# Two attention layers, a GRU and a last layer on one core: column tiles in the recurrent layer, a rebuilt variance in the last, one load moved up in the first

## The reference, cut to what matters

```
x = x + attention_0(x)          # 16 heads, softmax with mask
x = x + attention_1(x)          # 8 heads, queries are the keys
x = x + gru(h0=cond, inputs=x)  # 8 rows, 256 steps, width 512
    r = sigmoid(x_t W_r + b + h U_r + b);  z = sigmoid(x_t W_z + b + h U_z + b)
    n = tanh(x_t W_n + b + r * (h U_n + b)); h = (1 - z) * n + z * h
x = x + last(x, q=cond[1])
    blocks = x.reshape(8, 8 blocks, 32, 512).sum(axis=2)
    keys   = rms_normed(blocks @ Wk.T) * w;  a = softmax(keys @ q)
    proj   = (sum_n a_n blocks_n) @ Wo.T          # one row of 512 for each batch row
    y      = x + proj, then a layer norm over the 512 channels of every (batch, step)
```

## Time and profile before

| | us |
|---|---|
| median of 3 runs | 2085.04 |
| lowest, highest | 2074.66, 2086.17 |
| profiled execution: its own time | 2081.26 |
| profiled execution: span, first to last instruction | 2079.5 |
| attention, from 0 to the switch | 1006.5 |
| recurrent layer, 1006.5 to 2009.7 | 1003.2 |
| last layer, 2009.7 to the end | 69.8 |

### The profile page before, as it was taken

The page is one execution under the profiler, slowest core; times in us unless marked ns, Lnnn a source line. Parts: engine busy times, 40 slices in busy tenths (PEclk is TensorE's granted clock), DMA queues, the critical chain, the costliest instruction groups (busy, mean ns, idle before and its releaser), DMA issues. The chain is left out here.

```text
span 2079.5 us, 75171 instructions
## 1 busy us (share of the span) xinstructions
PE 1932.3 (93%) x32564; PEld 1312.7 (63%) x32564; DVE 1141.3 (55%) x3355; ACT 790.4 (38%) x2131; POOL 394.7 (19%) x867
## 2 busy tenths in 40 slices
PE   4788999999999999998899999999999999998777
PEld 2333444444444444444788888888888888887755
DVE  3535667575757566724255555555555555555546
ACT  0344555565646565653222222222222222222224
POOL 0011121111121202110212222212222221222103
PEclk7768999999999999997999999999999999999995
DMA  4525343442524251322300000000000000000002
GB/s 129 191 69 153 82 145 91 115 120 85 149 77 143 79 153 47 94 59 86 115 11 11 12 12 4 11 12 11 12 11 10 5 12 12 12 11 12 4 3 81
DMA packets 64616, 127.37 MB, mean 61 GB/s; under 512 B 14425, under 2 KB 21209, under 8 KB 60692
## 3 DMA queue, kind: packets, MB, share of 16 engines
q1 hardware_dynamic: 61212, 121.74, 19.9%
q0 software_dynamic: 3072, 0.82, 0.2%
HBM read 77.56 MB, written 37.85 MB: 55 GB/s over the span
## 5 line engine op out<-in xcount | busy, mean ns | idle before, releaser
L391 DVE TENSOR_REDUCE mx<-MX 128x1 f32<-128x512 f32 x768 | 486.6, 685 | 221.6 <-PE MX L511 221.0
L900 PE MATMUL gate<-whh,state 128*8 128x128 f32 x16384 | 496.3, 273 | 40.5 <-DVE state L823 28.9
L447 ACT ACTIVATE pr<-ST 128x512 f32<-128x512 f32 x768 | 412.2, 600 | 179.1 <-PE ST L531 178.2
L900 PEld LDWEIGHTS gate<-whh,state 128*8 128x8 f32 x16384 | 422.0, 91 | 89.6 <-DVE state L823 89.0
L511 PE MATMUL MX<-K,Q 51*128 51x512 f32 (+1 forms) x768 | 251.7, 478 | 25.7 <-DMA Q<-d_rows 19.5
L900 PE MATMUL pg<-whh,state 128*8 128x128 f32 x8192 | 270.8, 273 | 0.0
L801 DVE STREAM_TRANSPOSE trn<-gate 128x128 f32<-128x128 f32 x256 | 81.2, 317 | 338.1 <-PE gate L900 338.1
L852 ACT ACTIVATE rg<-pre 128x32 f32<-128x32 f32 x256 | 58.8, 230 | 541.4 <-DVE pre L803 541.3
L531 PE MATMUL ST<-Q,K 53*128 53x512 f32 (+1 forms) x768 | 247.0, 495 | 13.4 <-ACT pr L447 11.7
L531 PEld LDWEIGHTS ST<-Q,K 53*128 53x128 f32 (+1 forms) x768 | 101.2, 190 | 216.5 <-ACT pr L447 119.7
L900 PEld LDWEIGHTS pg<-whh,state 128*8 128x8 f32 x8192 | 223.7, 90 | 0.4
(11 more groups left out here) (166 smaller groups left out, 1940.9 us busy)
## 6 DMA issues: line engine op xcount, KB each, us to landing
d_q<-hi_q SPq DMA_DIRECT2D x32, 256.0 KB
d_q<-lo_q SPq DMA_DIRECT2D x32, 256.0 KB
d_k<-hi_k SPq DMA_DIRECT2D x32, 256.0 KB
d_k<-lo_k SPq DMA_DIRECT2D x32, 256.0 KB
K<-d_k SPq DMA_DIRECT2D x64, 128.0 KB
Q<-d_q SPq DMA_DIRECT2D x64, 128.0 KB
K<-d_k SPq DMA_DIRECT2D x16, 512.0 KB
Q<-d_q SPq DMA_DIRECT2D x16, 512.0 KB
```

Source lines behind the costliest of these rows:

```text
L391: dve.reduce_max(mx[:, u, col:col + 1], bank[:, :], AX.X).then_inc(mx_red, 1)
L447: act.activation(pr[:, kc % 2, i], ST[n % 3][:, :], ACT.Exp, scale=SCALE[UNITS[w][0]]).then_inc(exped, 1)
L900: last = pe.matmul(bank[32 * j:32 * j + B, lo:hi], held[q][:, c, :], whh[:, c, o + lo:o + hi], start=first, stop=done)
```

## The change

The diff, cut to its core:

```diff
--- before.py
+++ after.py
                     second_layer(it, 0)
-                else:
+                load_in(it + 2)
+                if not there(it):
                     sp.dma_start(xT[:], xt_in).then_inc(xT_in, 16)
                     preload(sp)
-                load_in(it + 2)
                 if there(it):
...
-        TG, TZ, RZ = 32, 16, 3
+        TG, TZ, RZ = 16, 16, 3
...
-        PIECES_Z = [(i, w, n) for i in range(TG // TZ) for w in range(C) for n in range(C)]
-        assert len(PIECES) == len(PIECES_Z) == TG
+        PIECES_Z = [(n, w, k) for n in range(1, NZ) for w in range(C) for k in range(C)]
+        Z_AT = [min(2 * t if t < TZ else TZ + t, len(PIECES_Z)) for t in range(T + 1)]
+        KEPT_Z = {next(t for t in range(T) if Z_AT[t + 1] >= C * C * n): n for n in range(1, NZ)}
+        T0 = T - TG
+        PARTS_AT, MEANS_AT = {T0 + 2 * n: n for n in range(last)}, {T0 + 1: 0, T0 + 3: 1, T0 + 6: 2}
+        CENTRE_AT = {T0 + 2 + n: divmod(n, C) for n in range(C * last)}
+        MU = (gb[1], zb, gb[1], gb[1])
...
+                pool.wait_ge(s_z_ev, 1)
+                pool.tensor_tensor(giZ[0][:], giZ[0][:], bz[:, 0], ALU.add).then_inc(s_z0, 1)
...
+                    if t in CENTRE_AT:
+                        blk, c = CENTRE_AT[t]
+                        dve.wait_ge(f_mu, blk + 1)
+                        dve.tensor_tensor(xa[:, blk, c], MU[blk][:, :], chunk(c, blk), ALU.add).then_inc(f_c, 1)
...
-                    last = pe.matmul(gb[i % 2][:, 0:TG * B], wih[:, n, i * P:(i + 1) * P],
-                                     xT[:, n, TG * blk:TG * (blk + 1), :].rearrange("p t b -> p (t b)"), start=n == 0, stop=n == C - 1)
+                    for j in range(4):
+                        last = pe.matmul(gb[i % 2][32 * j:32 * j + 32, 0:TG * B], wih[:, n, i * P + 32 * j:i * P + 32 * j + 32],
+                                         xT[:, n, TG * blk:TG * (blk + 1), :].rearrange("p t b -> p (t b)"), start=n == 0, stop=n == C - 1)
...
-                    i, w, n = PIECES_Z[k]
-                    t0 = TG * blk + TZ * i
-                    if w == 0 and n == 0 and t0 > 0:
-                        pe.wait_ge(s_z_ev, t0 // TZ)
-                    last = pe.matmul(zb[:, P * w:P * (w + 1)], xT[:, n, t0:t0 + TZ, :].rearrange("p t b -> p (t b)"),
-                                     wihZ[:, n, P * w:P * (w + 1)], start=n == 0, stop=n == C - 1)
-                    if w == C - 1 and n == C - 1:
+                def piece_z(n, w, k):
+                    if w == 0 and k == 0 and n > 0:
+                        pe.wait_ge(s_z_ev, n)
+                    for j in range(4):
+                        t0 = TZ * n + 4 * j
+                        last = pe.matmul(zb[32 * j:32 * j + 32, P * w:P * (w + 1)], xT[:, k, t0:t0 + 4, :].rearrange("p t b -> p (t b)"),
+                                         wihZ[:, k, P * w:P * (w + 1)], start=k == 0, stop=k == C - 1)
...
+                    if t == 0:
+                        pe.wait_ge(s_z0, 1)
+                    elif n > 0 and v == 0:
+                        pe.wait_ge(s_zd[n % RZ], 192 * (n // RZ + (0 if n % RZ == 0 else 1)))
...
+                        if n == 0:
+                            pe.matmul(psZ[t % 2][32 * j:32 * j + B, 0:P], identz[:, B * v:B * v + B], giZ[0][:, P * j:P * (j + 1)], start=True, stop=False)
+                            continue
...
-                        piece(blk + 1, k)
-                        piece_z(blk + 1, k)
+                        piece(blk + 1, 2 * k)
+                        piece(blk + 1, 2 * k + 1)
+                    for n, w, c in PIECES_Z[Z_AT[t]:Z_AT[t + 1]]:
+                        piece_z(n, w, c)
+                    if t in PARTS_AT:
+                        blk = PARTS_AT[t]
+                        if blk == 0:
+                            pe.wait_ge(s_gi_ev, PER * NG)
+                            pe.wait_ge(s_z_ev, NZ)
+                        else:
+                            pe.wait_ge(f_kept, blk)
+                        pe.wait_ge(s_acc, TB * (blk + 1))
+                        for c in range(C):
+                            mm = pe.matmul(gb[0][32 * c:32 * c + 32, :], mean[:, 0:32], chunk(c, blk), start=True, stop=True)
+                        mm.then_inc(f_part, 1)
+                    if t in MEANS_AT:
+                        blk = MEANS_AT[t]
+                        pe.wait_ge(f_kept, blk + 1)
+                        if blk == 2:
+                            pe.wait_ge(f_c, C)
+                        pe.matmul(MU[blk][:, :], fold[:], parts[:, blk], start=True, stop=True).then_inc(f_mu, 1)
...
+                def turn(blk):
+                    dve.wait_ge(f_var, blk + 1)
+                    if blk >= 2:
+                        dve.wait_ge(f_vf, blk - 1)
+                    dve.transpose(turned[:, blk % 2].rearrange("p w r -> p (w r)"), VB[blk % 2][:, :]).then_inc(f_vt, 1)
...
                 shift(0)
-                for c in range(C):
-                    centre(1, c)
                 shift(1)
-                for blk in range(NBLK):
-                    spread(blk)
-                    if blk + 2 < NBLK:
-                        for c in range(C):
-                            centre(blk + 2, c)
-                        shift(blk + 2)
-                    scale(blk)
+                turn(0)
+                shift(2)
+                spread(0)
+                turn(1)
+                scale(0)
+                shift(3)
+                spread(1)
+                turn(2)
+                scale(1)
+                spread(2)
+                turn(3)
+                scale(2)
+                spread(3)
+                scale(3)
...
+                def halves(bank, w):
                     for c in range(C):
-                        mm = pe.matmul(bank[32 * c:32 * c + 32, :], mean[:, 0:32], chunk(c, blk), start=True, stop=True)
-                    mm.then_inc(f_part, 1)
-                def means(blk):
-                    pe.wait_ge(f_kept, blk + 1)
-                    pe.matmul(MU[blk][:, :], fold[:], parts[:, blk], start=True, stop=True).then_inc(f_mu, 1)
-                pe.wait_ge(f_ld, 80)
+                        for j in range(2):
+                            mm = pe.matmul(bank[64 * j:64 * j + 64, 0:HD], br[:, c].rearrange("p n b -> p (n b)"), w[:, c, HD * j:HD * (j + 1)],
+                                           start=c == 0, stop=c == C - 1)
+                    return mm
...
                 def var(blk):
                     pe.wait_ge(f_sq, C * (blk + 1))
                     if blk >= 2:
-                        pe.wait_ge(f_sd, blk - 1)
-                    for g in range(4):
-                        for c in range(C):
-                            mm = pe.matmul(VC[blk % 2][:, g:g + 1], sq[:, blk % 2, c, g * P:(g + 1) * P], ones[:, 0:1], start=c == 0, stop=c == C - 1)
+                        pe.wait_ge(f_vt, blk - 1)
+                    for c in range(C):
+                        mm = pe.matmul(VB[blk % 2][32 * c:32 * c + 32, :], mean[:, 0:32], sq[:, blk % 2, c], start=True, stop=True)
                     mm.then_inc(f_var, 1)
+                def together(blk):
+                    pe.wait_ge(f_vt, blk + 1)
+                    o = 384 + W * blk
+                    pe.matmul(SP[0:32, o:o + W], pick32[:], turned[:, blk % 2, :, 0], start=True, stop=True).then_inc(f_vf, 1)
...
                 square(0)
                 square(1)
-                for blk in range(NBLK):
-                    root(blk)
-                    shifted_by_beta(blk)
-                    if blk + 2 < NBLK:
-                        square(blk + 2)
+                shifted_by_beta(0)
+                root(0)
+                square(2)
+                root(1)
+                shifted_by_beta(1)
+                square(3)
+                root(2)
+                shifted_by_beta(2)
+                root(3)
+                shifted_by_beta(3)
...
```

271 lines of the change are left out of this document (137 added, 134 removed).

## The result

The changed kernel takes 2053.16 us in the median of 4 runs (2046.30 to 2062.89), the kernel before 2083.41 in the same runs: ratio 0.987, interval 0.982 to 0.991. In two further sets it was 0.986 (0.984 to 0.988; 2050.80 against 2079.55 us) and 0.989 (0.987 to 0.991; 2060.13 against 2081.69). The profiled execution has 2051.92 us of its own and a span of 2050.1, 29.3 us less than before.

| stage | before | changed | difference | predicted |
|---|---|---|---|---|
| attention, up to the switch | 1006.56 | 990.15 | -16.4 | -10.0 |
| switch to the first scan | 24.72 | 19.86 | -4.9 | -8.6 |
| steps 0 to 15 | 61.60 | 64.32 | +2.7 | +2.2 |
| steps 16 to 254 | 915.36 | 917.32 | +2.0 | +0.6 |
| keys to `pm` | 19.10 | 12.45 | -6.7 | -5.5 |

What follows compares the result with a forecast made beforehand. It took an `xin` wait, pieces made ahead, the 3.83 us step chain and the last layer as limits. -10.0 - 8.6 + 2.8 - 5.5 - 10.1 = -31.4 us on 2081.3 gave 2050 us, range 2035 to 2067.

Steps and rivals of the forecast that it cites:

- Part 1: First layer: the load of `xin` issued earlier removes TensorE's whole 10.28 us wait; -10.0 us.
- bound of -11.5: First layer: the most the moved load was to gain, in us, as the low clock may rise earlier too.
- Rival B: First layer: TensorE later waits for a stack behind `xT`, giving back up to 10 us; 2060 us, chance 0.15.
- Part 2: Start of the recurrent layer: 48 groups of pieces at 0.26 us take 12.5 us instead of 21.1; -8.6 us.
- Part 3: Recurrent steps: +2.2 us in steps 0 to 15, +0.6 from three `means`; +2.8 us, bounds 0 and +6.
- 0.14 us a step: Steps 0 to 15: four groups and a longer `begin` take 1.24 us, 0.14 over the room; +2.2 us.
- The `means`: Steps 241, 243 and 246: wide products with 512 columns overrun the room by 0.2 us each; +0.6 us.
- Rival A: Recurrent layer: strips' weight loads run in series, a group costs 0.434 us; 2111 us, chance 0.05.
- Part 4: Last layer, keys to `pm`: a chain of 13.6 us in place of 19.1; -5.5 us, bounds -7.5 and -3.
- Part 5: Last layer, `pm` to last addition: walking DVE's and ACT's lists gives 36.9 us in place of 47.0; -10.1 us.
- rival D: Last layer: DVE's and ACT's list is longer than walked, 4 to 8 us less gain; 2056 us, chance 0.13.
- Clock C: Last layer: the clock stays up behind `pm` instead of falling to half; 2046 us, chance 0.10.

Runs made afterwards that it cites:

- e1: Kernel before the change with only the load of the next input moved ahead of xT and preload; 2066.60 us, ratio 0.993 to before.
- e2: Changed kernel with the old order of loads, so all of the change but the load's move; 2068.96 us, ratio 0.994 to before.
- e3: Changed kernel with the 3 MB load of the recurrent weights issued only once the first update block is kept; 2049.78 us in one run.
- e5: Changed kernel with the pieces in 128 weight columns again instead of strips, in steps of 16; 2054.79 us in one run.
- e9: Changed kernel with GpSimd's last-layer additions cut from 512 columns to 8, leaving out most of the last sum; 2056.62 us in one run.
- e6: Changed kernel with ScalarE's first root in the last layer ahead of the first quarter's beta additions; 2056.90 us in one run.
- a1: The changed kernel itself, measured again beside other experiments; 2060.13 us, ratio 0.989 to the kernel before.

## Why the prediction was right, and where its terms were off

The forecast was 2050 us, -31.4 on the profiled execution; it became -29.3, and the measured median, 2053, lies in the range. The mechanisms were those named, but the sizes of the five parts were off by 1.2 to 6.4 us, and three of the prediction's own signs failed: the stretch from the first update piece to the first selecting product took 15.8 us where 12.5 was forecast, steps before 16 took up to 4.59 us, and `pm` to the last addition took 40.9 us, with VectorE's longest waits (1.5 to 2.2 us) ahead of `scale` and not ahead of the first inverse (1.31).

**Part 1** (-10.0) named the wait and its end, and at equal time at the low clock it is -9.4. What came on top, up to -16.4 in one profile, goes with the clock. The bound of -11.5 for it was too tight: in the medians the load alone is worth 13.0 us and as the last of the parts 18.2, and in three profiles of one program the time at the low clock differs by 31 us and the switch by 9. Rival B did not happen: TensorE's later wait for `xin`, 5.55 us, was there before the change as well (5.16 us), and e1 (6.12) and e2 (3.10) have it too.

**Part 2** (-8.6) had the right rate, 0.26 us a group forecast and 0.23 measured in e3, and so the right work: with the holes of over 0.5 us taken off, the pieces take 12.1 to 12.3 us in the changed kernel's three profiles. It failed in taking the stretch for one without other limits: -5.2 up to the first state product. The prediction asked what `whh` does to the step that reads it, and not what else may be late while 3 MB move.

**Part 3** (+2.8) came out at +4.7. The 0.14 us a step for steps 0 to 15 does not exist: the first of them that are undisturbed take 3.83 us; others take 3.9 to 4.6, at places that differ between executions, and the sixteen take 0.8 to 3.8 us more than before over three profiles. e5, without the many instructions, has none of these, only its even 4.11. A fetch of code there is a guess. The `means` cost 0.08 each and not 0.2. The 2.0 us from step 16 on are these, 0.003 to 0.004 in each step, and three single steps (28, 109, 190) of 4.18 to 4.20, in every profile with the change. These three are not explained; e5 has them at the same places, so the number of TensorE's instructions is not what sets them. That drains go with strips was right and, as said, worth nothing. Rival A is out: sixteen strip instructions in 0.44 us.

**Part 4** (-5.5) became -6.7 (12.45 us, and 11.92 and 11.51 in the other two profiles): the keys took 2.60 us where 3.5 was taken, and the rest of the chain somewhat less.

**Part 5** (-10.1) became -6.1, and this is rival D at its foot. The walk of the two lists gave 36.9 us, and 36.6 is what e9 shows without GpSimd's work. The step that failed is that the shift and the two additions kept their durations from the earlier trace rows, where they had no such neighbour; 4.3 us is its price. The first root was one of the things that VectorE waits for (1.31 us, and e6 shows that 1.4 us hang on it). Clock C did not come: 0.50 from 2004.7 us on.

That the sum held is luck. The extra of Part 1 (-6.4) and of Part 4 (-1.2) stood against what Parts 2 and 3 lost (+5.6) and against GpSimd (+4.0). Parts 2 to 5 together came to -13.0 where -21.4 was forecast, and in the set of a1, with 21.6 us gained in all, the same kernel lies 10 us off the -31.4.

## What to carry to other kernels

Cost an instruction with the neighbours it will have: where VectorE and GpSimd both work on tiles in the work memory, a moved elementwise operation can take more than twice its time, and another order, not another operation, gets it back. Ask what a gain comes from before carrying its form along: here half the work ahead made the start shorter, and the strips that came with it cost some of that again. And when an engine idles and no engine releases it, set the packets of the instruction queue beside the idle time. Last, compare parts of a kernel by medians in one set and by stages at a like clock: one profile gave the load 16.4 us, the medians 13.0 to 18.2, the wait itself was 10.3.

## What the hardware showed that was not expected

- VectorE's addition of two tiles of 128 x 512 comes every 0.62 us alone, and GpSimd's every 1.24. Where both run all the time (2022.1 to 2025.4 us) each has one every 1.68 us. In strict turns it would be 1.86: the two nearly take turns. The 5.26 us for four shifts are a mean over such shifts and one that was alone.
- A TensorE hole of 2.1 to 3.0 us with no releaser, once or twice in each of ten profiles with strips and early weights, each beside a 16 KB packet of the instruction queue; none with the weights later or with a quarter of the instructions.
- In a row, sixteen instructions in strips take 0.46 us and the four wide ones in their place 0.48. In a step of 0 to 14 it is different: from the first selecting product to the next step's first state product it is 1.20 us with strips (e3) and 1.48 with wide pieces (e5), 0.1 us of it ahead of the first piece and the rest in the pieces. That is the 0.28 us between 3.83 and 4.11.
- One program's time at 1.2 GHz in the attention part: 113 to 143 us. The spread between its executions goes with it: of a1's six runs the two at 2052 and 2053 us have a mean granted clock of 0.961 and 0.962, the four at 2060 to 2061 us 0.953 to 0.956.
